# Column groups of the adjacency product reordered, each waiting for its own share of the scatters, and fewer scatters between the gathers

## The reference, cut to what matters

```python
edge_index = jnp.stack([src, dst])
x = x + _L0_gnn_ref(h, ..., src, dst, edge_type_8)      # attention, 4 heads, 8 relations
h = jnp.maximum(_layernorm(x), 0.0)
x = x + _L1_gnn_ref(h, edge_index, ...)                 # graph convolution:
    h = (x + sum(cluster_emb)) @ W
    deg = segment_sum(ones, dst); dinv = rsqrt(deg)
    out = segment_sum(h[src] * dinv[src] * dinv[dst], dst) + bias
    s = softmax(out, axis=1);  p = s @ cluster_emb;  return x + p
x = x + _L2_gnn_ref(...)                                # edge network and three dense layers
x = x + _L3_gnn_ref(...)                                # mean over neighbours, two products
```

## Time and profile before

| | before |
|---|---|
| time, median of 3 runs | 3186.56 us (3183.82 to 3191.64) |
| profiled execution: its own time | 3186.24 us |
| profiled execution: span of the core | 3184.4 us |
| mean granted TensorE clock | 0.932 of full speed |
| PE busy | 2844.6 us (89%) |
| DVE busy | 1838.6 us (58%) |
| ACT busy | 1403.1 us (44%) |
| POOL busy | 1015.7 us (32%) |

### The profile page before, as it was taken

The page is one execution under the profiler, slowest core; times in us unless marked ns, Lnnn a source line. Parts: engine busy times, 40 slices in busy tenths (PEclk is TensorE's granted clock), DMA queues, the critical chain, the costliest instruction groups (busy, mean ns, idle before and its releaser), DMA issues.

```text
span 3184.4 us, 48481 instructions
## 1 busy us (share of the span) xinstructions
PE 2844.6 (89%) x14970; PEld 1887.5 (59%) x15034; DVE 1838.6 (58%) x5217; ACT 1403.1 (44%) x3865; POOL 1015.7 (32%) x1048
## 2 busy tenths in 40 slices
PE   1789967999999889897879999799999999999998
PEld 1544437899999888886234444455555555545445
DVE  6577766888878666668144433255555555513334
ACT  1267766788777777783014000144444444401000
POOL 3166667777777777775000000000000000000000
PEclk6599988999999999995969999899999999999999
DMA  8966654333333333311934333300000000132232
GB/s 233 402 200 205 206 165 120 93 90 88 88 86 89 86 88 87 86 46 48 329 107 128 101 103 92 105 7 3 7 7 3 7 5 5 42 103 67 86 101 77
DMA packets 245032, 317.62 MB, mean 100 GB/s; under 512 B 121467, under 2 KB 162084, under 8 KB 240740
## 3 DMA queue, kind: packets, MB, share of 16 engines
q1 hardware_dynamic: 191412, 179.07, 19.9%
q0 software_dynamic: 49104, 104.11, 11.1%
q10 hardware_dynamic: 4320, 31.95, 2.5%
HBM read 237.42 MB, written 77.59 MB: 99 GB/s over the span
## 4 chain that ended last, share of the span: by engine, by line
PE 51%; DVE 23%; issue 8%; ACT 6%; DMA 5%; POOL 4%; DVEq 4%; SPq 0%; POOLq 0%
PE PS L1176 17%; PE PS L1021 15%; DVE SUMS L1589 4%; DMA BG<-a_d 3%; PE PS L987 3%; PE PS L844 3%; PE PS L962 3%; PE PS L1000 3%; ACT BG L675 3%; DVE BG L1725 2%; POOL BG L537 2%; DVEq L1604 2%; POOL a_d L528 2%; DVE OHB L1452 2%; DVE X L1595 2%
## 5 line engine op out<-in xcount | busy, mean ns | idle before, releaser
L528 POOL DMA_INDIRECT a_d<-VAL,IDXS x499 | 488.8, 980 | 219.4 <-issue 134.7
L1176 PE MATMUL PS<-BG,SL 128*128 128x512 f32 (+1 forms) x1440 | 535.8, 528 | 12.2 <-ACT SL L758 12.2
L537 POOL DMA_INDIRECT BG<-feat_d,IDXST x500 | 491.8, 984 | 153.4 <-issue 126.7
L675 ACT ACTIVATE BG<-BG,SL 128x64 f32<-128x64 f32 x2000 | 513.5, 337 | 0.0
L1589 DVE TENSOR_TENSOR SUMS<-SUMS,PS 128x640 f32 x500 | 409.2, 818 | 165.4 <-PE PS L962 150.0
L1176 PEld LDWEIGHTS PS<-BG,SL 128*128 128x128 f32 x1440 | 274.6, 193 | 251.0 <-issue 222.4
L569 POOL MEMSET BG<- 128x7680 f32 x1 | 6.5, 6500 | 1294.3 <-DVE MV L1856 1294.3
L962 PE MATMUL PS<-OHB,BG 128*128 128x128 f32 x2000 | 338.8, 293 | 0.0
L1000 PE MATMUL PS<-OHB,X 128*128 128x128 f32 x2000 | 319.4, 283 | 1.7 <-DVEq L1567 1.7
L1000 PEld LDWEIGHTS PS<-OHB,X 128*128 128x128 f32 x2000 | 289.4, 197 | 14.5 <-issue 1.7
L987 PE MATMUL PS<-W1A,X 65*128 65x256 f32 x1000 | 276.0, 399 | 3.9 <-ACT X L649 0.9
(11 more groups left out here) (299 smaller groups left out, 4179.1 us busy)
## 6 DMA issues: line engine op xcount, KB each, us to landing
BG<-a_d SPq DMA_DIRECT2D x171, 256.0 KB, 4.2
AL<-a_d SPq DMA_DIRECT2D x137, 256.0 KB, 2.6
a_d<-BG POOLq DMA_DIRECT2D x30, 1088.0 KB, 40.4
feat_d<-SUMS ACTq DMA_DIRECT2D x30, 1040.0 KB
BG<-rel_d SPq DMA_DIRECT2D x100, 160.0 KB
X<-in_edge_attr_dram SPq DMA_DIRECT2D x124, 128.0 KB
SUMS<-a_d SPq DMA_DIRECT2D x52, 256.0 KB, 2.6
SL<-key_d SPq DMA_DIRECT2D x50, 256.0 KB
```

Source lines behind the costliest of these rows:

```text
L528: pool.indirect_dma_start(a_d.rearrange("n (w o) -> (n w) o", o=1), bass.IndirectOffsetOnAxis(ap=IDXS[:, t:t + 1], axis=0), VAL[:, t:t + 1 ...
L537: pool.indirect_dma_start(RING[:, t // NB % 3, t % NB, :], None, feat_d.rearrange("n (r d) -> (n r) d", r=R), bass.IndirectOffsetOnAxis(ap ...
L675: last = act.activation(m, m, ACT.Copy, scale=EXT[:, b % 2, k, 1 + q:2 + q])
L1176: last = pe.matmul(PS[:, to + q, 0:width], lhs[:, i, c, :], w[:, c, q * width:(q + 1) * width], start=(c == 0), stop=(c == kc - 1))
```

## The change

It does four things.

1. Layer 2 takes its columns in another order (`GROUPS2`): 512..1535, 1536..2559, 2560..3583, then the first 512 columns, then the last 678. The edges' destinations are sorted, so low columns are reached by low edge tiles.
2. The scatters are cut into four runs (`CHUNKS` = 0, 200, 289, 425, 499) and each run has one of the four semaphores. DVE works out, from `BASE`, how many edge tiles begin below the end of each of the first three groups, and from that which runs the group needs (`NEED`, `NEEDI`). SP reads three numbers into registers ahead of each of these groups and waits for that much of runs 1 to 3, at least for 16 (one scatter); ahead of the fourth group it waits for all. POOL waits, behind the first scatter of runs 1 to 3, until it has landed, so that 16 always means that one.
3. Behind gather 85, two scatters come per five gathers in place of one per two.
4. The part for the first destinations moves to the end with its group: PE turns it inside the last group, and the 120 products with `FIRST` follow the last group.

The diff:

```diff
+        TILES = sb("TILES", [1, 3, 1])
+        NEED = sb("NEED", [1, 3, 3])
+        NEEDI = sb("NEEDI", [1, 3, 3], I32)
@@
+        OWN_G = 3
+        EARLY = OWN_G
+        GROUPS2 = [(512 + 1024 * g, 1024) for g in range(EARLY)] + [(0, 512), (512 + 1024 * EARLY, N - 1024 * EARLY)]
+        assert len(GROUPS2) == len(GROUPS) and 0 < N - 1024 * EARLY <= 1024
+        CHUNKS = [0, SOON] + [1024 * (g + 2) * T // N + 16 for g in range(EARLY - 1)] + [TR]
+        CHUNKED = [CHUNKS[k + 1] - CHUNKS[k] for k in range(4)]
+
+        def chunk_of(t):
+
+            return max(k for k in range(4) if t >= CHUNKS[k])
@@ SP
-                n, (c0, w) = adj(p, g, t), GROUPS[g]
+                n, (c0, w) = adj(p, g, t), (GROUPS if p else GROUPS2)[g]
@@
-            for k in range(4):
-                sp.wait_ge(a_set[k], 16 * len(range(k, TR, 4)))
             sp.wait_ge(s("dve_mark"), DVE_MARKS["y_ready"])
-            adjacency_from(0, 0, every)
+            for g in range(len(GROUPS)):
+                if g < EARLY:
+                    _, need = nc.values_load_multi_w_load_instructions(
+                        NEEDI[0:1, g, :], engines=[mybir.EngineType.SP], min_val=16, max_val=16 * max(CHUNKED[1:]))
+                    sp.wait_ge(a_set[0], 16 * CHUNKED[0])
+                    for k in range(1, 4):
+                        sp.wait_ge(a_set[k], need[k - 1])
+                elif g == EARLY:
+                    for k in range(4):
+                        sp.wait_ge(a_set[k], 16 * CHUNKED[k])
+                adjacency_from(0, g * NT, (g + 1) * NT)
@@ POOL
-                ).then_inc(a_set[t % 4], 16)
+                ).then_inc(a_set[chunk_of(t)], 16)
+                if t in CHUNKS[1:4]:
+                    pool.wait_ge(a_set[chunk_of(t)], 16)
@@
-                if t >= LEAD and (t - LEAD + 1) * 1 // 2 > (t - LEAD) * 1 // 2:
+                if t >= LEAD and (t - LEAD + 1) * 2 // 5 > (t - LEAD) * 2 // 5:
                     scatter_late(counted)
@@ PE
-            for g, (c0, w) in enumerate(GROUPS):
+            for g, (c0, w) in enumerate(GROUPS2):
                 if g >= 2:
                     pe.wait_ge(s("d_free"), g - 1)
                 if g == 2:
                     pe.wait_ge(s("deg_sb"), 8)
-                    for b in range(LB):
-                        last = turn(PS[0:LT, 7, b * K3:(b + 1) * K3], VBK[:, b * LT:(b + 1) * LT], K3)
-                    last.then_inc(s("pe_mark"), 1)
                 for t in range(NT):
+                    if g == OWN_G + 1 and t == 4:
+                        pe.wait_ge(s("d_free"), OWN_G + 1)
+                        for b in range(LB):
+                            last = turn(PS[0:LT, 7, b * K3:(b + 1) * K3], VBK[:, b * LT:(b + 1) * LT], K3)
+                        last.then_inc(s("pe_mark"), 1)
@@
-                if g == 2:
+                if g == OWN_G + 1:
                     pe.wait_ge(s("dve_mark"), DVE_MARKS["own_ready"])
                     for t in range(NT):
                         for b in range(LB):
@@
-                while g >= 2 and (turned + 1) * P <= GROUPS[g - 1][0] - 512:
+                while g >= 2 and (turned + 1) * P <= 1024 * (g - 1):
@@ DVE
+            for g in range(EARLY):
+                step(ts(BROW, BASE[:, :], 1024.0 * (g + 1), 0.0, ALU.is_lt, ALU.add, accum_out=TILES[:, g, :]))
+            for k in range(1, 4):
+                last = ts(NEED[:, :, k - 1:k], TILES[:, :, :], float(CHUNKS[k]), 16.0 * (CHUNKED[k] - 1), ALU.is_gt, ALU.mult)
+            step(last)
+            step(ts(NEED[:, :, :], NEED[:, :, :], 16.0, None, ALU.add))
+            step(cp(NEEDI[:, :, :], NEED[:, :, :]))
@@
-                for g, (c0, w) in enumerate(GROUPS):
+                for g, (c0, w) in enumerate(GROUPS2):
...
-                    if g == 0:
-                        step(cp(VBK, v[:, 0:512]))
-                    o = 512 if g == 0 else 0
-                    cp(ACC[0:K3, 1, c0 + o - 512:c0 + w - 512], v[:, o:w]).then_inc(s("d_free"), 1)
-                    if g == 1:
+                    to = VBK if g == OWN_G else ACC[0:K3, 1, c0 - 512:c0 + w - 512]
+                    cp(to, v[:, 0:w]).then_inc(s("d_free"), 1)
+                    if g == OWN_G:
```

## The result

| | before | after |
|---|---|---|
| time, median | 3186.52 us (3183.82 to 3191.64, 4 runs) | 3155.97 us (3152.64 to 3158.84, 4 runs) |
| ratio to before, 95% interval | | 0.9901 (0.9888 to 0.9913) |
| profiled execution: its own time | 3186.24 us | 3158.84 us |
| span of the core | 3184.4 us | 3156.7 us |
| mean granted TensorE clock | 0.932 | 0.936 |

The change makes the kernel 30.6 us faster (1.0%). The forecast was 51.5 us, and 3156 lies 4 us above the end of its range.

What follows compares the result with a forecast made beforehand. The prediction took POOL to bound the loop's last nine batches. Its terms, -42.8 - 5.8 - 7.8 + 2.6 + 2 = -51.8 us against the profiled 3186.2, gave 3134.4, as a median 3135 us; range 3126 to 3152.

Steps and rivals of the forecast that it cites:

- Term 1: Loop: gathers come earlier, so late batches take 34.0 us without waiting for them; -42.8 us.
- Rival B: Loop: something other than gathers holds late batches at 35.9 us; gain 28 us, time 3150; chance 0.16.
- D: Loop: not freed, ACT or PE being as late as the gathers; time 3177.6 us; chance 0.04.
- Term 2: Start of layer 2's product: no longer held by scatters, less 2 us for a register load; -5.8 us.
- Term 5: Product's first two groups: some 27 scatters run beside the loads, at most 0.26 us each; +2 us taken.
- its last sentence: Product: the prediction is wrong if the last scatter's 122 writes stop the loads around 1500; no size or chance.
- the bound of 0.26 us per scatter: Loads beside scatters: the most one scatter costs them, from 2.1 us left over nine scatters; 7 us in all.
- Terms 3 and 4: Layer 2's product: new column groups, -7.8 us; products with `FIRST` and turns behind the last group, +2.6 us.
- Rival C: Product's loads: each tiny scatter write takes a load's turn, 21.6 us in place of 2; time 3155; chance 0.08.
- Rival E: Product: loads and scatters block each other; 3189 us, or 3224 if the scatters also slow down; chance 0.04.
- The clock: Loop: the granted TensorE clock, 0.88 in the mean in every second late batch, stays at 1.00 through them.

Runs made afterwards that it cites:

- experiment 1: The changed kernel with all 122 fillers of the last scatter writing to different rows: 3135.68 us, ratio to before 0.9841.
- experiment 5: The changed kernel, fillers still on one place, but their scatter issued second in the last run, POOL waiting for the last values: 3136.79 us, ratio to before 0.9834.
- two halves: The kernel before with only the new groups and their waits: 3189.38 us, ratio 1.0011; with only two scatters per five gathers: 3193.01 us, ratio 1.0016.
- a third edit: The last scatter's fillers spread over different rows, on top of the changed kernel: 3135.68 us, ratio to before 0.9841.

## Why the prediction was wrong, point by point

- **Term 1, the loop: right in size** (-42.8 forecast, -41.2 measured), in part by luck. No `soft_in` behind 1055 waits for gathers; the last one is at 1329.88 (forecast 1329.4), the last gather at 1316.13 (1317.3). But a late batch takes 34.1 to 34.8 us, 34.45 in the mean, where 34.0 was taken; with the rest of the loop that makes the gain 38.1. The other 3.1 us come from ahead of the late batches: before, the batch from 871.6 to 914.0 took 42.4 us, with the clock low for 13.7 us from 890 on, and the changed kernel's trace has no such batch. Nothing in the edit was found to explain that. Rival B, a batch of 35.9, fell, and so did D.
- **Term 2, the start of the product: right** (-5.8 forecast, -6.0 measured). The register load takes 1.9 us where 2 were taken: `y_ready` is there at 1457.17, the first load goes at 1459.07.
- **Term 5 is the step that failed.** The prediction had the last scatter land at 1511.5 and charged that to those who wait for it only, and for the loads beside it "I take **+2**". The row behind it showed loads beside scatters with distinct places, and for these it held: the first group lost nothing. But the last scatter was not of that kind. Its 122 writes to one place all but stopped the loads from about 1502 to 1519, and that cost 20.2 us in the second group (44.0 in place of 23.8). Experiments 1 and 5 show that it is this scatter and its places. The 19.56 us of its landing stood in the rows, and the prediction said that the trace doesn't tell whether the fillers make it so late; it gave the case no price and no chance among the rivals, though its last sentence named it. A rival "the last scatter stops the loads while it lands", 19.56 less the few us that the loads in flight cover, at about 3135 + 17 = 3152, could have been worked out from the earlier trace rows alone. Two smaller things in this term: the last scatter started at 1496.61, not 1491.9, because the landing waits took 8.4 us and not 5.4, and because of the slower scatters beside L1644, which no row had shown. And the bound of 0.26 us per scatter is 2.1 / 9 = 0.23; beside distinct places it is hardly anything: the first two groups of experiment 1 took 48.3 us with 25 scatters beside them, where 47.6 were reckoned without.
- **Terms 3 and 4, the narrower groups and the end, were mis-sized.** The 512 columns took 14.6 us and the last 678 some 18.9 with the turns inside, where 13.0 and 15.8 were forecast, 4.7 more; the 120 products and the turns took 5.1 where 4.8 were. In experiment 1, without the stall, these two groups take 14.2 us at a DMA share of 0.85 and some 17 at 0.94:

```profile
1535.60:1549.80 14.20, 11.13 (x31) 2.69 (x30) 0.67 (x1) 0.00 (x0) 0.00 (x0) 0.88 0.85 256
1550.80:1567.70 16.90, 13.28 (x64) 3.72 (x62) 1.24 (x6) 0.00 (x0) 0.00 (x0) 1.00 0.94 301
```

  256 GB/s and 301, against 328 in the wide first group: narrower loads in the same ring of seven ran at a lower rate. The pace of 0.43 us per load of before was a lower bound, not the rate in between. Why they are slower, and whether more buffers would mend it, was not tried.
- **Rival C** had the right time (3155) by the wrong mechanism: turn by turn, the first group would have suffered first, and it moved 332 GB/s beside 17 scatters. The Trainium skill ("DMA: Bandwidth & Descriptors", "SWDGE vs HWDGE vs iDMA") says that each DMA engine takes turns between its internal queues; that each small write would thereby cost a load's turn was the prediction's own step, and this trace doesn't show it for writes to distinct places. **Rival E** had the two block each other in general, which experiment 1 excludes. Its remark that it decides from 0.3 us more per scatter on can't be worked out again: 27 x 0.3 = 8 us would have left the time at 3143, inside the range.
- **The clock** did as forecast, 1.00 through the late batches.

With 20.2 in place of the +2, and about 5 for the narrower groups, the prediction's own sum gives 3158; 3158.8 was measured in the profiled execution, and 3156.0 in the median.

## What to carry to other kernels

Before a wait for scatters or gathers is taken off a path, look at how long each lands and what it writes: one that takes eight or nine times as long to land as its neighbours is not only late, it can hold the transfers that will now run beside it. Padding that sends many lanes of an indirect write to one place is the first suspect; give each filler a place of its own, or issue that scatter where nothing else loads. And where several waits hold the same instruction, none of them alone shows its worth: here two halves gave 0 each, together 31 us, and with a third edit 51.

## What the runs showed of the hardware that was not expected

- An indirect DMA of 128 values of 2 bytes lands 2.1 us after its start when its places are distinct, and 17.5 to 19.6 us after it when 122 of them share one place, with no load beside it. Each further write to the same place adds 0.13 to 0.16 us. What serialises them inside the DMA or the memory these runs don't tell. Writes to different places of one row, or close to each other, were not tried, so "the same place" may be narrower than what matters.
- While such writes go on, loads issued from another engine's queue stand still on the whole: 361 GB/s before, 9 to 38 during, 367 after, with a DMA share of 0.62 to 0.99, all of it the loads' own packets. A busy share of the DMA is thus no sign that bytes move. The loads here all read the matrix that the scatter writes; whether loads of another tensor would be held is not shown. Later scatters of the same queue are held as well (experiment 5).
- Scatters to distinct places, one each 1.3 to 1.6 us, cost loads at 328 to 332 GB/s nothing that shows. They themselves land later beside loads: after 4.6 us in the median, where it is 2.1 without them.
- A scatter takes POOL 1.29 us in place of 0.96 while DVE runs L1644 (bf16 out of f32, 125x640). Only the coincidence in time is shown.
- The same dense stage, with the same instructions, takes 729.6 to 737.3 us in fourteen traces, by how long the granted clock stood at its lower level in it (10.2 to 23.9 us).
